# The mixer's decay differences: two 512-column products with one constant stationary operand in place of eight 128-column products with eight

## The reference

```python
# per head h (8 of them), width 16 each; A * dt is the log decay of each row
A_cs  = cumsum(A*dt)                       # along time, within a chunk
Lmat  = exp(A_cs[l] - A_cs[s])  for l >= s # the decay from row s to row l
Y_diag = einsum('bcln,bcsn,bhcls,bcshp->bclhp', C, B, Lmat, X)
Y_off  = C @ state_in * exp(A_cs)          # state carried from chunk to chunk
y = Y_diag + Y_off + x * Dskip
```

## Time and profile before

| | |
|---|---|
| Time, median of 3 runs | 3345.88 us (3342.76, 3345.88, 3358.94) |
| Profiled execution: span, first to last instruction | 3382.6 us |
| Instructions in it | 62340 |
| VectorE busy | 2933.7 us, 87% |
| ScalarE busy | 2463.6 us, 73% |
| GpSimd busy | 1642.2 us, 49% |
| Mean granted clock of TensorE | 0.907 |

### The profile page before, as it was taken

One profiled execution on the slowest core, in us unless ns is written; L12 is line 12 of the kernel. 1 busy time (PEld: TensorE's weight loads), 2 busy tenths in 40 slices (PEclk: granted clock), 3 DMA queues, 4 the chain that ended last, 5 costly groups with the idle time before them and its releaser, 6 DMA issues. The chain is left out here.

```text
span 3382.6 us, 62340 instructions
## 1 busy us (share of the span) xinstructions
PE 2884.2 (85%) x13152; PEld 1671.5 (49%) x13152; DVE 2933.7 (87%) x6964; ACT 2463.6 (73%) x7615; POOL 1642.2 (49%) x1196
## 2 busy tenths in 40 slices
PE   4799889998889889988888998898888677888958
PEld 2454444454444445444444444444444344677743
DVE  5999999999999999999999999999999556676546
ACT  3888888888888888888888888888888523332214
POOL 1455555555555555555555555555555424222104
PEclk7999999999999999999999999999999867677659
DMA  4444444444444444444444444444444100000001
GB/s 124 135 133 126 136 130 130 130 132 126 132 129 136 127 134 129 130 134 132 132 132 130 132 132 134 132 134 126 134 130 127 48 17 10 16 7 4 0 7 45
DMA packets 293411, 356.42 MB, mean 105 GB/s; under 512 B 24850, under 2 KB 239956, under 8 KB 293204
## 3 DMA queue, kind: packets, MB, share of 16 engines
q1 hardware_dynamic: 291076, 351.66, 35.3%
q10 hardware_dynamic: 2128, 2.85, 0.3%
HBM read 140.00 MB, written 169.87 MB: 92 GB/s over the span
## 5 line engine op out<-in xcount | busy, mean ns | idle before, releaser
L855 DVE MAX8 top<-work 128x8 f32<-128x512 f32 x1536 | 978.5, 677 | 0.0
L952 POOL TENSOR_SCALAR kept<-scores,top 128x512 f32<-128x512 f32 x256 | 489.9, 1914 | 540.0 <-DVE top L855 535.5
L865 DVE MATCH_REPLACE8 work<-top,work 128x512 f32<-128x512 f32 x1024 | 682.7, 673 | 0.0
L556 PE MATMUL bank<-keys_of_head,qt 128*128 128x512 f32 x1024 | 598.2, 669 | 0.0
L541 PE MATMUL bank<-probs_t,u 128*64 128x512 f32 x2048 | 467.7, 599 | 4.0 <-POOL u L916 3.6
L852 DVE MAX8 top<-scores 128x8 f32<-128x512 f32 x512 | 327.4, 679 | 99.8 <-issue 83.9
L916 POOL TENSOR_TENSOR u<-raw,inverse 128x512 f32<-128x512 f32 x192 | 200.2, 1043 | 433.1 <-ACT raw L746 433.1
L958 POOL TENSOR_TENSOR probs_of_tile<-kept,exps 128x512 f32<-128x512 f32 x256 | 326.6, 1276 | 61.1 <-POOL kept L952 53.7
L560 PEld LDWEIGHTS bank<-relj,identity 128*128 128x128 f32 x1024 | 210.4, 206 | 285.7 <-issue 276.9
L788 ACT ACTIVATE exps<-scores,nmax 128x512 f32<-128x512 f32 x512 | 341.7, 714 | 8.3
L865 DVE MATCH_REPLACE8 work<-top,scores 128x512 f32<-128x512 f32 x512 | 341.3, 673 | 0.0
(11 more groups left out here) (259 smaller groups left out, 5594.2 us busy)
## 6 DMA issues: line engine op xcount, KB each, us to landing
rel_scratch<-rel SPq DMA_DIRECT2D x256, 383.0 KB, 3.8
relj<-rel_scratch SPq DMA_DIRECT2D x256, 256.0 KB, 2.8
probs_scratch<-probs_of_tile SPq DMA_DIRECT2D x256, 256.0 KB, 2.5
band<-probs_scratch SPq DMA_DIRECT2D x256, 256.0 KB, 3.6
pair_j<-table_j SPq DMA_DIRECT2D x64, 257.0 KB, 2.9
xt<-stream_normed_t SPq DMA_DIRECT2D x64, 256.0 KB, 3.0
pair_o<-table_o SPq DMA_DIRECT2D x64, 67.0 KB, 2.4
experts_xs<-stream_normed_t SPq DMA_DIRECT2D x16, 256.0 KB, 2.3
```

The lines of the kernel that those rows point to most:

```text
L556: nc.tensor.matmul(SC[h][:, :], qt[bpar][:, Tb * P:(Tb + 1) * P], t.kz[bpar][h][:, :], start=True, stop=False)
L855: nc.vector.max(top[q][:, h, 8 * r:8 * r + 8], work[:, h, :]).then_inc(s.next_tops, 1)
L865: nc.vector.match_replace(out=work[:, h, :], in_to_replace=top[q][:, h, 8 * r:8 * r + 8], in_values=sc[q][:, h, :] if r == 0 else work[:, ...
L952: nc.gpsimd.tensor_scalar(kept[:, :], sc[q][:, 1, :], top[q][:, 1, TOPK - 1:TOPK], None, ALU.is_ge).then_inc(s.at_least, 1)
```

## The change: what it does

In `first_half` the eight products of a tile, each with its own stationary operand al[q][:, h, :] and the moving operand upto, become two. Each has the constant `after` as its stationary operand and four heads of `al` beside each other, 512 columns, as its moving operand, and fills one bank of DF. In `spread` GpSimd multiplies upto in place of after, so that al[q][k, h, l] = a[k, h] * upto[k, l]. The sum over k is the same one. Semaphores, buffers, banks and the order of the lists stay as they are.

```diff
@@ first_half (tensor)
                 pe.wait_ge(m.spread, t + 1)
                 if not early(t):
                     pe.wait_ge(m.exps, t)
-                for h in range(MH):
-                    last = nc.tensor.matmul(DF[h // 4][:, (h % 4) * P:(h % 4 + 1) * P], al[q][:, h, :], r.upto[:, :],
+                for e in range(2):
+                    last = nc.tensor.matmul(DF[e][:, :], r.after[:, :],
+                                            al[q][:, 4 * e:4 * e + 4, :].rearrange("k h t -> k (h t)"),
                                             start=True, stop=True)
                 last.then_inc(m.diffs, 1)
@@ spread (gpsimd)
-                nc.gpsimd.tensor_tensor(al[q][:, :, :], bcast(r.after[:, :], [[0, MH], [1, P]]),
+                nc.gpsimd.tensor_tensor(al[q][:, :, :], bcast(r.upto[:, :], [[0, MH], [1, P]]),
                                         b.a[:, bass.ds(t * MH, MH)].unsqueeze(2).to_broadcast([P, MH, P]),
                                         ALU.mult).then_inc(m.spread, 1)
```

## The result

| | before | after |
|---|---|---|
| Median of 20 runs each, us | 3345.75 | 3359.74 |
| Lowest to highest, us | 3327.27 to 3358.94 | 3334.65 to 3368.41 |
| Ratio after/before, 95% interval | | 1.0038 [1.0021, 1.0054] |
| Profiled execution's span, us | 3382.6 | 3366.7 |

The account below looks back on a forecast made before the run. The prediction took TensorE to bound the mixer, busy 313.7 of 365 us. The tiles' gain of 0.9 us, with removed loads and other edits at 0, took the median from 3345.9 to 3345.0 us, range 3332 to 3360.

Parts of the forecast that it names:

- The tile's cost: L1490 in each mixer tile: 3.62 us unchanged at 1.2 GHz, 1.95 to 1.88 at 2.4 GHz, a gain of 0.07 us.
- the 3 us named: Sign in the mixer's trace: TensorE's matmul time stays within 3 us at the same clock.
- I am wrong if: Four matmuls under 3.4 us at 0.50; mixer clock outside 0.64-0.70, same steps; mixer over 2.2 us shorter, steps unchanged.
- The removed loads: Weight loads at L1490: 69 us of load time goes, costed at nothing because matmuls stream in the meantime.
- Rival 1: Weight loads are on the mixer's TensorE path after all: 38 us less, 3308 us; chance 4%.
- rival 4: Mixer slower because weight loads counted for the clock: 21 us in L1490 alone, 3366 us or more; chance 3%.
- so it should flip few steps, in either direction: Mixer tile c=2: spread comes 0.07 us forward at the high clock, so few steps change kind, 6.5 us each.
- two margins (0.99 and 0.47 us): At tile c=2, GpSimd's spread leads VectorE's state decay by 0.99 us in one case, trails by 0.47 in the other.
- single runs lie 16 us apart: Three earlier runs of the kernel spanned 16.2 us, 3342.8 to 3358.9, two and a half steps that change kind.
- Rival 3: Short mixer steps become long as the spread at c=2 leads VectorE's state decay: 3358 to 3365 us; chance 11%.
- price of 6.5 us a step: Mixer steps without the meeting take 38.1 and 38.8 us, with it 45.2 and 44.3: about 6.5 us a step.
- the sum of durations (0.9 us): Mixer's whole gain: 12.3 tiles' worth at the high clock times 0.07 us, 0.9 us, all else 0.

Follow-up runs that it names:

- fill kernels: Four mixers alone, old and new form, L1509's products widened to 128 columns plus three unread 512-column products a step: 1390.70 and 1382.29 us.
- four mixers: Kernel without attention and both expert stages, mixer run four times: old form 1575.21 us, new form 1594.26; repeated, 1580.56 and 1582.08.
- four traces above: Uneven-clock traces of the mixer run four times without attention and experts, two old form (1575.21, 1580.56 us), two new (1594.26, 1582.08 us).
- m4_old_defer: Four mixers alone, old form, GpSimd's spreads for the next step held back until VectorE has the new state: 1564.63 us.
- m4_four256: Four mixers alone, four products of 256 columns a tile with `after` stationary, between old and new form: 1595.16 us.
- m4_swap8: Four mixers alone, operands exchanged as in the change but still eight products of 128 columns a tile: 1584.48 us.
- wide kernels: Four mixers alone, old and new form, L1509's products given 128 columns in place of 16: 1422.94 and 1433.60 us.
- m4_new_fill: Four mixers alone, new form, L1509's products widened to 128 columns plus three unread 512-column products a step: 1382.29 us.
- m4_new_pad1: Four mixers alone, new form, with one more unread product of 128 columns at tile c=3 of each step: 1573.47 us.
- full_new_defer: Whole kernel, new form, GpSimd's next spreads waiting for VectorE's state of tiles c=0 and c=1: 3344.68 us, ratio 0.9984 to the kernel before.
- m4_new2: Repeat of the four mixers alone in the new form, two products of 512 columns a tile: 1582.08 us.
- m4_old: Kernel without attention and both expert stages, mixer run four times in the old form, eight products a tile: 1575.21 us.
- m4_new: Kernel without attention and both expert stages, mixer run four times in the new form, two products a tile: 1594.26 us.

## Why the prediction was wrong

**The tile's cost was right.** Four matmuls take 1.88 us at 2.4 GHz, as forecast, and 3.62 at 1.2 GHz, with the next line 3.41 us behind the first start, the pitch of before (TensorE in order of time, after):

```profile
3018.12 3.62 PE L1490 MATMUL bank<-mixer_a_spread,rest_after 128*128 128x512 f32 x4
3021.53 0.42 PE L1498 MATMUL bank<-identity,mixer_x 128*128 128x128 f32 x1
```

The 0.07 us a tile shows as 0.06 where the clock is held high, and the matmul time of the mixer stayed within the 3 us named. In the fill kernels, where the steps are steady, the change is a gain of tenths of a microsecond a step. None of the signs named under "I am wrong if" came out; they had none for steps that go over to the longer kind.

**The removed loads are worth nothing, as forecast.** 55 us less load time in the mixer (69 was forecast; the line's own fell by 60.5), and no time came of it. Rival 1 is out. The pitch of 81 and 131 ns that the Trainium skill gives ("TensorE: Matmul & The Clock Gate", section "Back-to-back issue gap") speaks for a gain; the trace after does not agree, with 1.88 us for four matmuls of 512 columns at the high clock, 0.47 each.

**The removed loads did not cost clock.** The mixer's clock went from 0.68 to 0.69 with 384 loads fewer: rival 4 is out.

**What failed is one step: "so it should flip few steps, in either direction".** It compared 0.07 us with two margins (0.99 and 0.47 us) read at two steps, took what was left for scatter without a side, and so put the flipped steps at nothing in the sum; the change cost 14 us in the medians, and in the trace three more steps had the meeting. Two things were wrong in it. First, 0.07 us is a shift within one tile at one clock, while the spread moved by 2.9 and 1.5 us against the decay in the two steps above, 1.2 and 1.3 us of it because the differences of c=2 ran in 1.88 us where they had taken 3.09 and 3.15, and the rest because TensorE stood elsewhere against VectorE when they began. In the trace after all six later steps have the meeting, where three had none before. The margins were those of steps in one phase of the clock, not a property of the kernel. That the start of a step decides this, and carries the sum of all that ran before it, the stretch before the mixer too, is the likely reason and is argued, not shown: no run varied the start alone. Second, that single runs lie 16 us apart was read as a reason for expecting nothing; it was a sign that small shifts are multiplied. With the clock held the four mixers' runs lie 9 and 6 us apart, without it 16 to 43 (with one or three products added, though, 5 and 3).

Rival 3 named the place, and its condition (the differences of c=2 at 2.4 GHz) is what the traces show. Its 11% was too little. Holding the spreads back takes the meeting away and 0.38% becomes 0.06%, so the meeting seems to have a part in the loss; but the waits also move the steps against the clock, and one product more a step reached 1573 us with 14 meetings left in. Its price of 6.5 us a step was wrong: it was read at two pairs of steps. The three new meetings cost 2.1 to 2.7 us each, and over the four traces above it is 2.5 us in the mean, about the wait itself. Long steps come without a meeting as well (up to 43.5 us in m4_old_defer). The meeting itself is VectorE's decay at 0.27 us alone and at 1.77 us beside GpSimd's two-input multiplication, where it ends 0.14 us behind that one (2929.75 and 2929.61). The Trainium skill has this as a lock ("SBUF — State Buffer", section "SBUF: two separate sides"): a VectorE instruction with two inputs in SBUF and a GpSimd one that reads SBUF exclude each other. The traces agree; it says nothing of the place in a step where that costs 2.1 to 3.0 us of TensorE.

**What stays open** is why the shift goes to the slow side in the mean. In the whole kernel it does, in 20 runs against 20. In four mixers by themselves it was 19 us and then 1.5, with 26 meetings for old and 25 for new in the traces. m4_four256 came out 11 us above m4_swap8, measured beside it. So "the new form meets oftener" is seen in one execution of each whole kernel and is not shown as a rule. In the pair of wide kernels, with a better clock and with 2 and 4 meetings, the medians lie 10.7 us apart on the slow side, and the ratios' intervals overlap. A story in which 0.07 us always tips a step the wrong way would fit the 0.38% and not the rest.

## What to carry to other kernels

Where a trace shows the same step at two lengths, with the clock or a meeting of two engines between them, price a small edit by what it does to the phase, and widen the chances on both sides: the sum of durations (0.9 us) was right as a sum, and what happened was 14 times as large and of the other sign. Take the coupling away first (a wait that keeps the two engines apart, work that holds the clock), and only then measure small savings, since without it 0.07 us a tile can't be seen as what it is. Read the price of such a meeting from many steps, not from two. Fewer weight loads are no gain in themselves where, as here, 128 columns stream beside each.

## What the runs showed of the hardware

- Up to 128 columns beside a full weight load were nearly free. Sixteen matmuls of 16 columns take 1.86 us at 2.4 GHz, and of 128 columns 1.95 us, in m4_new_fill:

```profile
479.97 1.95 PE L1518 MATMUL bank<-mixer_dtx,mixer_weights 128*128 128x128 f32 x16
```

- With those added columns the granted clock of the four-mixer kernel in the old form was 0.839 where it had been 0.695, and its time 152 us less than 1575. Three products more a step that nothing reads took it to 0.898 and 1391 us. In the whole kernel the two are worth 1.5%, the largest gain of this study, and it comes from work that nothing needs.
- With one product of 128 columns more a step that nothing reads (m4_new_pad1) the runs of the four mixers lay 5 us apart, where those of the new form without it lay 21 and 43 us apart, in five or six runs each.
- Many of the steps' lengths come again to a tenth of a microsecond or so in different executions (37.3 us in the trace after, in full_new_defer and in m4_new2; 44.3 before and after, 44.4 in m4_old, m4_new and m4_new2).
